# A twelve-block decoder on one core: order of products in the shared-key attention, one ScalarE sum of absolute weights, and two load queues in the narrow-head attention

## The reference

```
0  L0 attn   16 heads of 16, causal, biases on q, k, v and output
1  L0 xattn  selective state space over 256 steps, 16 states
2  L0 ffn    8 experts, the best one per token
3  L1 attn   16 heads that share one key/value head of 128: scores = v_lin k_lin^T / 128,
             every head is the same, so one head is computed with the sum of the 16 output weights
4  L1 xattn  state space
5  L1 ffn    ternary weights: needs mean(|w_out|) over 1024x256 weights, then a gated product
6  L2 attn   differential attention: 2 x 16 heads of 8, causal
7  L2 xattn  16 heads of 128, keys and queries normalised
8  L2 ffn    product keys, top 8
9  L3 attn   16 query heads of 128, one shared key/value head, softmax((x Wq + bq) k^T) v, @ Wo + bo
10 L3 xattn  16 query heads, 8 key/value heads
11 L3 ffn    recurrent thought, gate, layernorm
```

## Time and profile before

| | |
|---|---|
| median of 3 runs | 2325.41 us (2319.49 to 2339.16) |
| the profiled execution | 2325.68 us, of it 2324.1 us from first to last instruction |
| PE busy | 1876.4 us (81%) |
| DVE busy | 1376.0 us (59%) |
| ACT busy | 891.9 us (38%) |
| POOL busy | 312.4 us (13%) |
| mean granted TensorE clock | 0.860 of full speed |

### The profile page before, as it was taken

One profiled execution on the slowest core, in us unless ns is written; L12 is line 12 of the kernel. 1 busy time (PEld: TensorE's weight loads), 2 busy tenths in 40 slices (PEclk: granted clock), 3 DMA queues, 4 the chain that ended last, 5 costly groups with the idle time before them and its releaser, 6 DMA issues.

```text
span 2324.1 us, 28947 instructions
## 1 busy us (share of the span) xinstructions
PE 1876.4 (81%) x10350; PEld 1296.8 (56%) x10350; DVE 1376.0 (59%) x2540; ACT 891.9 (38%) x2118; POOL 312.4 (13%) x269
## 2 busy tenths in 40 slices
PE   5764769674735576689899988997999999999997
PEld 3442444432422344566666756885566675666665
DVE  3358975958989582456666416885466514555425
ACT  1246520336523104456666215551455404444200
POOL 2122530003530203311111000000000000000001
PEclk9785559665557798999999989997999999999979
DMA  4010010010010111000001020000000100002000
GB/s 117 8 37 0 1 33 28 5 57 1 0 46 0 19 23 48 2 21 14 16 14 63 1 82 1 1 1 1 10 9 11 48 1 19 14 14 64 1 1 18
DMA packets 25741, 49.16 MB, mean 21 GB/s; under 512 B 6262, under 2 KB 19603, under 8 KB 24092
## 3 DMA queue, kind: packets, MB, share of 16 engines
q1 hardware_dynamic: 25644, 47.85, 6.9%
HBM read 42.20 MB, written 1.05 MB: 19 GB/s over the span
## 4 chain that ended last, share of the span: by engine, by line
PE 57%; DVE 27%; issue 7%; ACT 5%; SPq 2%; POOL 1%; DMA 1%; DVEq 0%; ACTq 0%; POOLq 0%; PEldq 0%
PE banks L1268 7%; PE banks L1331 7%; DVE big L953 6%; PE banks L1302 6%; PE banks L1343 5%; PE banks L1323 3%; DVE big L573 3%; PE banks L1585 2%; PE banks L2202 2%; PE banks L480 2%; PE banks L1995 2%; PE banks L1974 2%; PE banks L491 2%; ACT big L2101 2%; DVE big L1679 1%
## 5 line engine op out<-in xcount | busy, mean ns | idle before, releaser
L1420 DVE COPY arena<-banks 128x512 f32<-128x512 f32 x196 | 135.3, 690 | 259.7 <-PE banks L1323 256.0
L1331 PE MATMUL banks<-arena,big 128*128 128x256 f32 x784 | 217.6, 400 | 9.0 <-DVE arena L1420 8.9
L1302 PE MATMUL banks<-big 128*128 128x256 f32 x784 | 209.7, 391 | 1.6 <-ACT big L1457 1.6
L1483 ACT ACTIVATE arena<-banks,arena 128x256 f32<-128x256 f32 x392 | 193.3, 501 | 20.3 <-DVE arena L1375 17.1
L1501 ACT ACTIVATE big<-banks 128x256 f32 (+1 forms) x196 | 75.3, 384 | 275.0 <-PE banks L1331 275.0
L1268 PE MATMUL banks<-x_feat,arena 128*128 128x512 f32 x392 | 178.2, 598 | 1.2 <-ACT big L1467 1.2
L1331 PEld LDWEIGHTS banks<-arena,big 128*128 128x128 f32 x784 | 139.7, 191 | 66.6 <-DVE arena L1420 52.5
L227 POOL TENSOR_TENSOR ln_rstd<-ln_var_eps,neg_half 128x2 f32<-128x2 f32 x48 | 37.5, 781 | 963.3 <-DVE ln_var_eps L207 963.3
L1375 DVE TENSOR_REDUCE arena<-banks 128x2 f32<-128x512 f32 x196 | 134.3, 686 | 41.1 <-PE banks L1302 41.0
L1302 PEld LDWEIGHTS banks<-big 128*128 128x128 f32 x784 | 134.4, 191 | 28.2 <-issue 14.5
L953 DVE TENSOR_TENSOR_SCAN big<-big,banks 128x1024 f32<-128x1024 f32 x64 | 145.7, 2279 | 0.0
(11 more groups left out here) (312 smaller groups left out, 3361.2 us busy)
## 6 DMA issues: line engine op xcount, KB each, us to landing
big<-big SPq DMA_DIRECT2D x32, 64.0 KB, 2.3
arena<-in_L0f_w SPq DMA_DIRECT2D x1, 2048.0 KB, 8.3
arena<-in_L1a_wo SPq DMA_DIRECT2D x1, 2048.0 KB
arena<-in_L1f_gv SPq DMA_DIRECT2D x1, 2048.0 KB
arena<-in_L2a_qk_w SPq DMA_DIRECT2D x1, 2048.0 KB
big<-big SPq DMA_DIRECT2D x64, 32.0 KB
arena<-in_L2x_wo SPq DMA_DIRECT2D x1, 2048.0 KB
arena<-in_L2x_q_w SPq DMA_DIRECT2D x16, 128.0 KB, 2.0
```

What stands on the lines that cost most here:

```text
L1302: last = mm(ps[:, h * SEQ:(h + 1) * SEQ], q[:, b * SEQ + h * P:b * SEQ + (h + 1) * P], k[:, b * SEQ:(b + 1) * SEQ], start=not self.mask, s ...
L1331: last = mm(slot, self.v[:, 2 * b + kc, :], self.probs_t[:, u % 2, kc, :], start=(kc == 0), stop=(kc == 1))
L1420: v.tensor_copy(self.probs_t[:, u % 2].rearrange("p a b -> p (a b)"), B[4 + u % 2][:]).then_inc(self.turn_read, 1)
L1483: last = a(self.probs[:, u % 2, h, :], B[2 + u % 2][:, h * SEQ:(h + 1) * SEQ], ACT.Exp, bias=self.neg_max[:, u % 2, h:h + 1], scale=scale, ...
```

## The change

It touches four things.

1. Block 0's start: `qk_w` and the 16 copies of `qk_b` are issued by ACT on its own queue; SP's queue holds `x_feat` and the constants first, and `x_tok`, `ctx_feat` and the rest later. Waits are split (`feat_loaded`, `qk_loaded`, `w_loaded`, `b_loaded`; `prepared` counts each pair of copies). DVE fills `k` with ones at once, ahead of its copies, and the four copies of a row of ones are gone. POOL adds the output bias to `x_tok` only after `v_ready`.
2. Both narrow-head blocks: ACT issues the moves of the first keys itself, between staging `blk` 0 and `blk` 1; all moves wait for `cleared` 3 (`q`, `v` and `k` filled) where they waited for 1. The second score pass starts per group, and score_t(0) stands ahead of the last turn of maxima. In sum_up the product that needs no mask comes first.
3. Shared-key heads: keys, queries, two scores, then values. The value bias is added by ACT as it writes `out` (Identity with a bias in place of Copy), the output bias by one DVE addition on `x_tok` as the block begins (loaded to all 128 partitions). 8 + 8 bias products fall away in each of blocks 3 and 9.
4. The weight sum: one ACT instruction with an accumulator, issued in block 2 after the gate's exponentials; the DVE scan is gone.

```
 SmallHeads.sync / scalar
-        for dst, src in loads:
-            sp.dma_start(dst, src).then_inc(self.w_loaded, 16)
-        e.wait_x_feat(sp, l)
-        sp.wait_ge(e.consts_made, 1)
-        sp.wait_ge(self.k_cleared, 1)
-        for j in range(4):
-            row = 32 * j + w
-            sp.dma_start(self.k[row:row + 1].rearrange("o g t -> o (g t)"), e.ones[0:TILES * self.groups, :]).then_inc(self.moved[0], 16)
+        for blk, s in ((0, 0), (1, 1), (1, 0)):
+            self.move(sp, blk, s)
+            if g >= 2:
+                sp.wait_ge(self.rows_moved[g % 2], 64 * (g // 2))
+        if not self.diff:
+            act.dma_start(self.qk_w, d[n + "_qk_w"].rearrange("g p s c f -> p g s c f")).then_inc(self.qk_loaded, 16)
+                    act.dma_start(self.qk_b[row:row + w, blk, :], d[n + "_qk_b"][32 * j:32 * j + w, g, :]).then_inc(self.b_loaded, 16)
+            act.wait_ge(self.b_scaled, 1)
...
+            if blk == 0:
+                self.move(act, blk, 1)
 SmallHeads.tensor
-            if u == 0:
-                pe.wait_ge(self.rows_moved, 16 * 4 * G)
-            if u >= self.slots:
+            if b == 0:
+                pe.wait_ge(self.rows_moved[g % 2], 64 * (g // 2 + 1))
+            if u < self.slots:
+                pe.wait_ge(self.maxed, self.units - self.slots + u + 1)
+                pe.wait_ge(self.max_read, G - self.slots + 1 + u)
+            else:
-            for half, kc, first in ((0, 0, True), (1, 0, True), (1, 1, False)):
+            pe.wait_ge(self.exped, 2 * u + 2)
+            for half, kc, first in ((1, 0, True), (0, 0, True), (1, 1, False)):
+                if half == kc and not self.hosts:
+                    pe.wait_ge(self.masked, 2 * u + 2)
 SmallHeads.vector
-        nc.vector.memset(self.k, 0.0).then_inc(self.k_cleared, 1)
+            nc.vector.memset(self.k, 1.0).then_inc(self.cleared, 1)
 WideHeads.tensor / vector / scalar
-                                    mm(out, e.x_feat[:, c, tok], self.kv_w[:, c, DH:2 * DH], start=(c == 0), stop=False)
-                                last = mm(out, e.ones[0:1, :], self.v_b, start=False, stop=True)
+                                    last = mm(out, e.x_feat[:, c, tok], self.kv_w[:, c, DH:2 * DH], start=(c == 0), stop=(c == CH - 1))
-            produce(0, 0, ["v", "k"], first={"v": 0, "k": 2})
-        produce(0, 0, self.takes(0))
+            produce(0, 0, ["k", "q"], first=self.first)
         score(0, 0)
         score(0, 1)
+        if self.kv == "shared":
+            produce(0, 0, ["v"], first=self.first)
+            pe.wait_ge(self.proj_read, 6)
-            if self.bias:
-                last = mm(e.y_bank(t), e.ones[0:1, :], self.o_b, start=False, stop=True)
+        if self.bias:
+            dve.wait_ge(e.xt_psum, 4 * self.l)
+            ch.link(dve, v.tensor_tensor(e.x_tok[:], e.x_tok[:], bcast(self.o_b, 1, TILES), ALU.add))
-        if self.aside:
-            self.aside.scan(dve)
 RunningSums
-        self.e.nc.scalar.activation(self.w, self.w, ACT.Abs).then_inc(self.absolute, 1)
+        self.e.nc.scalar.activation(self.w, self.w, ACT.Abs, accum_out=self.e.lane_sums[:, 0:1]).then_inc(self.e.lanes_summed, 1)
```

191 lines of the change are left out of this document (95 added, 96 removed).

## The result

| | before | changed |
|---|---|---|
| median | 2327.2 us (4 runs) | 2240.59 us (4 runs, 2235.2 to 2243.05) |
| ratio | | 0.9629, 95% interval 0.9597 to 0.966 |
| profiled execution | 2325.68 us | 2239.59 us, span 2237.9 us |
| mean granted TensorE clock | 0.860 | 0.876 |

What follows compares the result with a forecast made beforehand. The prediction took the wait ending last at each touched place, not engine shares, as the bound. Terms for blocks 0, 6, 3 and 9 summed to 94.2 us, taking 2325.7 to 2231 us; forecast 2219 to 2243, outer ends 2212 and 2260.

Steps and rivals of the forecast that it cites:

- a: Block 0's start: reordered loads and preparation let PE start at 11, first scores 13.1 us earlier.
- rival C: Block 0's start: POOL's fills hold DVE's packing copies, PE starts at 15 instead of 11; 2235 us, chance 0.13.
- b: Block 0's second score pass: earlier exponentials 6.1 us, six units at full clock 8.2; 14.3 us won.
- c: Block 6's moves: 16 copies on each of two queues instead of 32 on one; 10.5 us won.
- Rival B: Block 6's moves: two queues don't issue side by side, the gain falls to 1 us; 2241 us, chance 0.10.
- d: Block 6's second score pass: unit 4 starts at 889.1 instead of 896.68; 7.6 us won, low end 5.
- rival A: Score pass changes, blocks 0 and 6: clock falls all the same, costing 8.2 and 2.7 us; 2242 us, chance 0.20.
- e: Block 3: scan gone, new product order, fewer bias products; 33.2 us won, 24.7 of it at the first transposes.
- f: Block 9: earlier transposes 11.5 us, dropped output bias products 5.0, ACT's Identity costing 1; 15.5 us won.
- Rival D: Blocks 3 and 9: the values run at half clock, costing 4.4 us in each; 2240 us, chance 0.05.
- Rival E: Block 9's loop: clock does not come up ahead of it, 120 us more; 2351 us, chance 0.02.

Runs made afterwards that it cites:

- fills_first: Changed kernel with POOL's two fills of block 0 moved to the head of its program; ratio 0.9630 against the kernel before.
- before_again: The kernel before, unchanged, profiled once more; run once, no ratio; block 0 took 40.87 us from last turn of maxima to last score_t.
- pass_old: Changed kernel with the old start of the second score pass in both narrow-head blocks; ratio 0.9657 against the kernel before.
- moves_sp: Changed kernel with all moves on SP's queue again; ratio 0.9657 against the kernel before.
- loads_late: Changed kernel with SP holding block 7's loads until unit 12 of block 6's second pass is read; ratio 0.9629 against the kernel before.

## Why the prediction was right, and where it was not

The time, 2240.59, is 10 above the 2231 forecast and inside the range. The sum is off by 8.1 and hides two larger errors, which cancel in part: about +9 from a part of the kernel that I had taken for better known than it was (shared-key heads), and -17 in all from the rest, most of it from block 6's second pass and from blocks that nothing touched.

- **a (13.1 forecast, 10.8 measured).** The mechanism held, and rival C happened, to which I gave 0.13: POOL's fills held the copies. fills_first shows it. The step that failed is "with POOL's preparation 9.5 ... I take 11": the row of 4.519 for a copy beside an addition was read as a danger for the forecast and not as its likeliest course, though the fills and the copies were both due at 10. ACT's queue was no limit: its bias loads took 0.59 each.
- **b (14.3, 14.9).** Right in both halves for this pair of profiles: 6.6 up to unit 2 (6.1 forecast) and 8.3 behind it (8.2). That the clock falls at the pause agrees with the runs: all four passes with the old start had a fall here. Its length is not: the 8.2 for "six units at 2.38 instead of 3.74" was read from one profile, whose fall lasted 31 us, and in the other three it lasted 7. From unit 2 on `before_again` took 30.9 and the changed kernel 30.8. So the second half was luck with the profile of before. The condition "if the clock holds" was met, as it was in five of ten profiles. The new order of products in sum_up gave 0.3 at most (`before_again` 40.87, `pass_old` 40.55).
- **c (10.5, 11.2).** Right: 16 issues on each queue side by side, ACT's second staging behind its moves, the scores at 25.5 behind the projection (25.6 by the forecast), 9.2 earlier than before, and 2.0 more in the first score pass. "No row shows what issuing costs on ACT": it was 0.80 in block 6 and 0.59 to 0.64 in block 0. Rival B is ruled out by moves_sp.
- **d (7.6, -1.4).** The step that failed is the clock: in the profiled execution it fell for 20 us at the pass change, as rival A had it with a chance of 0.20. The forecast's 889.1 for unit 4 is 9.2 behind the last turn, and where the clock stays up it is 8.8 (`loads_late`); here it was 11.9. Rival A gave this 2.7, where a fall costs 7.3 to 8.7, since it lasts longer than the units that were counted. The low end of 5 allowed for no such fall. Of the -1.4, 1.1 were won in the pass and 2.5 lost behind its last score_t, which no experiment took apart.
- **e (33.2, 36.9).** Right in mechanism: the scan set the start. The transposes come 15.7 behind the start of the block where 17.8 was forecast, so 24.8 earlier within it (22.7); the start itself came 2.1 earlier (2), which the 24.7 of the forecast holds as well. 1.9 where I had 1.5 for the units in between, and 8.1 where I had 7 from the output product on. DVE's addition, 2.29, and sum were covered.
- **f (15.5, 20.5).** Three sizes. The start gave 13.7 (11.5 forecast): the values took 3.73, not 5.0, and began 1.8 behind the scores' start, not 2.8; keys and queries took 9.3 (9.2). The output products gave 6.8 (5.0): a tile with its bias product came every 7.73, without it every 6.94, so a product cost 0.79 and not 0.69 less an overlap; no experiment put the output bias back by itself. ACT's Identity showed nothing above 0.3 (1 taken). That the rows, and not the order, made the start slow was not seen; 12.5 of the 13.7 are theirs.
- **Rival D** did not happen: the values ran at full clock in both blocks. **Rival E** did not: the loop took what it took before.
- **Blocks that nothing touched gave back 5.5.** Of it 3.3 are in block 11, whose stretch from 2179.74 to 2222.64 took 42.90 with the clock at 0.50 from 2186.5 to 2193.0 and PE busy without a pause; it took 39.6 in `before` and nine others, and some 42.9 in four profiles in all. Block 4 and block 7 took about 1 more each. No term of the forecast allowed for any of it.

## What to carry to other kernels

Units that come out 1.6 times as long behind a pause say that the clock was low in that execution, and for how long in that one only: the same pause was followed by 7 us at 0.50 in one profile and by 31 in another of the same kernel. Before pricing "the clock will stay up", take a second profile of the same kernel, count the pause and the slow units apart, and read the granted clock itself, since a fall that lies half in the pause hardly shows in the units. Two queues are worth having where a stage issues dozens of small copies, and the last of them is what the next stage waits for; check that the engine with the second queue has nothing due behind them. Products of a row of ones for a bias are dearer than their rows say if they stand behind an idle stretch: add the bias where the result is read anyway.

## What the runs showed of the hardware that was not expected

- Eight DVE copies of 128x128 float32 took 7.11 us beside two POOL fills of 3.51 and 3.65, and 1.17 without them. A DVE fill beside a POOL fill took 3.47, no longer than alone. The rule that the forecast quoted for rival C from the Trainium skill (SBUF — State Buffer, Who interferes with whom) is borne out for a fill, which the rows before had not shown.
- TensorE at 94 to 100% busy stayed at the 1.2 GHz level for the 15 us in which one-row products stood between its 128x128 products, and reached the 2.4 GHz level within 4 us when they did not.
- The granted clock fell to 0.50 at every one of eight pass changes at which PE stood idle for some 4.2 us, and for 20 to 24 us in five of ten score passes of block 6 with no pause above 0.75 us around the change. In block 11 it was at 0.50 from 2186.5 to 2193.0 with no pause at all.
- An issue of a 32 KB copy took 0.67 on SP alone, 0.73 on SP and 0.80 on ACT side by side, and 0.53 on POOL as a third. POOL's twelve copies landed 2.6 to 9.4 us after their issue, the later ones the later, and PE went on 9.4 us behind SP's last issue.
